# Graph attention and a small network on one core: 32 hidden outputs in column quarters of TensorE, half the heads of the last 23 tiles on DVE, and part of the network's start moved into those tiles

## The reference

```python
h = layernorm(x)
q, k, v = h @ Wq + bq, h @ Wk + bk, h @ Wv + bv        # 8 heads of 64
logits = sum_d(q[src] * k[dst]) / 8 + edge_bias        # rows = src, cols = dst
att = softmax of logits over the edges of one row
y = segment_sum(att * v[dst], src)
x = x + y @ Wo + bo
# the small network, two pipelines (add, sub), two positions
g = layernorm(x)                # 11 of its columns become features
r = relu(relu(f @ W0 + b0) @ W1 + b1) @ W2 + b2        # 160 wide, 2 outputs
x = x + (x + one-hot codes made of r at columns 128 to 160)
```

## Time and profile before

| | |
|---|---|
| median of 3 runs | 3393.04 us (3389.54 to 3396.01) |
| the profiled execution, its own time | 3388.5 us |
| its span, first to last instruction | 3386.7 us, mean granted TensorE clock 0.941 |
| busy | PE 2965.5, DVE 2891.4, ACT 2207.6, POOL 2206.9 us |
| sorting, projections | to some 1170 us |
| the tiles | to 2976 us |
| the network | to 3386.7 us |

### The profile page before, as it was taken

The page is one execution under the profiler, slowest core; times in us unless marked ns, Lnnn a source line. Parts: engine busy times, 40 slices in busy tenths (PEclk is TensorE's granted clock), DMA queues, the critical chain, the costliest instruction groups (busy, mean ns, idle before and its releaser), DMA issues.

```text
span 3386.7 us, 50546 instructions
## 1 busy us (share of the span) xinstructions
PE 2965.5 (88%) x11485; PEld 1732.4 (51%) x11610; DVE 2891.4 (85%) x8827; ACT 2207.6 (65%) x7734; POOL 2206.9 (65%) x2509
## 2 busy tenths in 40 slices
PE   6898888888887369999999999999999999889998
PEld 4554544544554135555555555555555555445554
DVE  9897777777776379999999999999999999867776
ACT  6332222222221059999999999999999999934443
POOL 0377777777777557777777777777777777511110
PEclk9898888888898689999999999999999999999999
DMA  6343333333332688878888887888888888411121
GB/s 205 81 135 102 106 107 100 102 101 107 104 104 67 224 287 256 253 253 254 256 257 254 257 259 252 258 258 253 257 256 252 257 256 259 145 66 69 68 70 55
DMA packets 258890, 615.16 MB, mean 182 GB/s; under 512 B 69451, under 2 KB 80023, under 8 KB 258338
## 3 DMA queue, kind: packets, MB, share of 16 engines
q0 software_dynamic: 144832, 443.72, 41.5%
q1 hardware_dynamic: 107414, 155.39, 15.1%
q10 hardware_dynamic: 6348, 12.80, 1.1%
HBM read 550.28 MB, written 61.49 MB: 181 GB/s over the span
## 4 chain that ended last, share of the span: by engine, by line
POOL 26%; DVE 25%; issue 20%; PE 14%; DMA 8%; ACT 3%; DVEq 2%; another core or an unknown queue 1%; ACTq 0%; SPq 0%; POOLq 0%
POOL rec_scratch L617 22%; DMA big<-kv_scratch,small 8%; DVE big L1374 6%; PE banks L1920 5%; DVE small L1272 5%; DVE big L1266 5%; PE banks L1949 4%; POOL big L638 3%; ACT big L799 3%; POOL small L645 2%; DVE big L992 2%; PE banks L1963 1%; PE banks L1874 1%; PE banks L1823 1%
## 5 line engine op out<-in xcount | busy, mean ns | idle before, releaser
L799 ACT ACTIVATE big<-big,small 128x65 f32<-128x65 f32 x6656 | 1625.9, 339 | 4.8
L638 POOL DMA_INDIRECT big<-kv_scratch,small x832 | 842.8, 1013 | 405.6 <-DVE small L1272 285.7
L617 POOL DMA_INDIRECT rec_scratch<-big,small x782 | 770.0, 985 | 340.4 <-issue 237.9
L1874 PE MATMUL banks<-big,small 128*128 128x260 f32 x3328 | 898.4, 393 | 96.1 <-POOL small L645 42.7
L1823 PE MATMUL banks<-big,small 128*128 x1664 | 876.5, 609 | 30.7 <-DMA big<-q_scratch 12.0
L1874 PEld LDWEIGHTS banks<-big,small 128*128 128x128 f32 x3328 | 597.4, 190 | 534.4 <-ACT big L799 243.0
L1374 DVE SCALAR_TENSOR_TENSOR big<-big,loS,banks 128x520 f32 x832 | 611.4, 735 | 20.2 <-PE banks L1874 18.6
L1731 PE MATMUL banks<-big 128*128 128x512 f32 (+1 forms) x1176 | 609.5, 666 | 19.5 <-DVE big L982 19.5
L1266 DVE TENSOR_TENSOR big<-banks,big 128x512 f32<-128x512 f32 x832 | 558.6, 671 | 43.9 <-PE banks L1823 25.7
L645 POOL TENSOR_SCALAR small<-iotaF,small 128x128 f32<-128x128 f32 x832 | 524.3, 630 | 54.1 <-PE banks L1874 28.2
L1272 DVE TENSOR_REDUCE small<-big 128x8 f32<-128x512 f32 x832 | 548.4, 664 | 0.0
(11 more groups left out here) (257 smaller groups left out, 2742.1 us busy)
## 6 DMA issues: line engine op xcount, KB each, us to landing
rowR<-lo_rows SPq DMA_DIRECT2D x97, 256.0 KB
big<-src_rows SPq DMA_DIRECT2D x97, 256.0 KB, 3.6
big<-in_x_dram SPq DMA_DIRECT2D x96, 256.0 KB, 2.8
big<-kv_scratch,small POOLq DMA_INDIRECT x832, 5.2
rec_scratch<-big,small POOLq DMA_INDIRECT x782
kv_scratch<-big SPq DMA_DIRECT2D x48, 260.0 KB
q_scratch<-big SPq DMA_DIRECT2D x48, 256.0 KB
kv_scratch<-big SPq DMA_DIRECT2D x48, 256.0 KB
```

What stands on the lines that cost most here:

```text
L617: e.indirect_dma_start(recd, bass.IndirectOffsetOnAxis(ap=ridx[:, c % 4, j:j + 1], axis=0), rec[:, 8 * c + j, :], None).then_inc(s_sc[c % ...
L638: e.indirect_dma_start(KV[:, vat(t):vat(t) + YW + D], None, KVd, bass.IndirectOffsetOnAxis(ap=recB[b_ % 4][:, t % 16, 9:10].bitcast(i32), ...
L799: ins = e.activation(heads(Vr(t), h, h + 1), heads(Vr(t), h, h + 1), ACT.Copy, scale=ph[:, h:h + 1])
L1874: ins = e.matmul(YB[t % 2][:, i, :], oh[t % 4], Vr(t)[:, 260 * i:260 * i + 260], start=True, stop=True)
```

## The change

1. **Last 32 outputs.** Part two of layer two is made as four products of 128 columns for each weight, each into 32 partitions of bank 5 (the column quarters of the array). So `h2[1]` holds all four groups at partitions 32 j, ACT's relu there has 128 columns instead of 512, and the weights of the outputs, `N2t`, have one block of four columns for each quarter with zeros elsewhere (1114 columns of `fwd` instead of 1102, six more `wload`).
2. **Last 23 tiles (809 to 831).** ACT scales heads 4 to 7 (`HV = 4`); heads 0 to 3 are one DVE product of 128x260 (`pv`), and `yt` waits for both.
3. **The network begins in them.** `f_y` of windows 0 to 5, `f_yT` of 0 to 5, `f_yTe` of 0 to 4, `f_xb` of 0 to 3, `f_wo` and `f_x1` of 0 and 1 are put at fixed steps of the tiles' loops. `f_wo` of 2 and 3 stay behind the last tile. SP loads after `yt` of tile 809. The network's buffers are laid into slots of the k and v ring that are free by then.

Three products of 512 columns became twelve of 128 columns with 32 outputs. The diff, cut to its core:

```diff
-        fwd = dram("network_weights", (128, 1102), f32)
+        fwd = dram("network_weights", (128, 1114), f32)
+        LAST = T - DEL
+        HV = 4
...
-                wload(W2t[0:32, 4 + 2 * pi_:6 + 2 * pi_], wT[2, 128:160, 100:102])
+                for j in range(4):
+                    wload(W2t[32 * j:32 * j + 32, 4 + 4 * j + 2 * pi_:6 + 4 * j + 2 * pi_], wT[2, 128:160, 100:102])
...
 (SP)
-            q.wait_ge(s_ya, T)
-            q.wait_ge(s_yt, T)
-            q.wait_ge(s_pva, T)
-            e.dma_start(fw2, fwd).then_inc(s_fw, 16)
-            e.dma_start(WoS, wo.rearrange("(c p) n -> p c n", p=128)).then_inc(s_wo, 16)
-            for w in range(XR):
-                f_load(w)
+            q.wait_ge(s_yt, T - 22)
+            q.wait_ge(s_rd, T)
+            q.wait_ge(s_pr, T)
+            f_load(0)
...
+            f_load(1)
+            f_load(2)
+            f_load(3)
+            e.dma_start(fw2, fwd).then_inc(s_fw, 16)
+            f_load(4)
+            f_load(5)
+            f_load(6)
+            q.wait_ge(s_yt, T - 20)
+            f_load(7)
...
 (POOL)
+                if s - T in (10, 13, 16, 19):
+                    f_xb((10, 13, 16, 19).index(s - T))
...
 (ACT)
-                for h in range(8):
+                for h in range(HV if t >= LAST else 0, 8):
...
+                if s - T in (10, 12, 16, 19, 22):
+                    f_yTe((10, 12, 16, 19, 22).index(s - T))
...
+                    e.activation(h2[1][0:C // 4, 0:128], BK[5][0:C // 4, 0:128], ACT.Relu).then_inc(s_h2r, 1)
...
 (DVE)
+            def pv(t):
+                v = Vr(t)[:, 0:65 * HV].rearrange("p (h d) -> p h d", d=65)
+                q.wait_ge(s_ex, t // 16 + 1)
+                e.tensor_tensor(v, v, pB[t // 16 % 2][:, t % 16, 0:HV].rearrange("p (h a) -> p h a", a=1).broadcast_to([128, HV, 65]), ALU.mult).then_inc(s_pvv, 1)
...
+                if LAST <= s - DEL < T:
+                    pv(s - DEL)
+                if s - T in (7, 8, 11, 13, 17, 20):
+                    f_y((7, 8, 11, 13, 17, 20).index(s - T))
+                if s - T in (15, 18):
+                    f_x1((15, 18).index(s - T))
...
-            for w in pair(0) + pair(1) + pair(2):
-                f_y(w)
-            for w in pair(0):
-                f_x1(w)
...
 (PE)
+                q.wait_ge(s_pvv, t - LAST + 1)
...
+                if s - T in (8, 10, 14, 17, 20, 23):
+                    f_yT((8, 10, 14, 17, 20, 23).index(s - T))
+                if s - T in (12, 15):
+                    f_wo((12, 15).index(s - T))
...
+                    for j in range(C // 128):
+                        ins = e.matmul(BK[5][32 * j:32 * j + 32, 0:128], lw[:, 128:160], h1[i][:, 128 * j:128 * j + 128],
+                                       start=(i == 0), stop=(i == 2))
...
+                        e.matmul(BK[7][0:n, 4 * j:4 * j + 4], h2[0][:, c0:c0 + n], N2t[:, 0:4], start=True, stop=False)
+                        ins = e.matmul(BK[7][0:n, 4 * j:4 * j + 4], h2[1][:, 0:n], N2t[:, 4 + 4 * j:8 + 4 * j], start=False, stop=True)
...
+            f_wo(2)
+            f_wo(3)
             f_fq(0)
```

More of the change, by code:

```diff
@@ L863, in _ @@
             q.wait_ge(s_ya, T)
[L864 to L868 removed]
+            q.wait_ge(s_fw, 39 * 16)
+            f_yTe(5)
             for w in pair(0):
                 f_root(w)
[L871 to L872 removed]
             f_FT(0)
```

184 lines of the change are left out of this document (89 added, 95 removed).

## The result

| | before | changed |
|---|---|---|
| median of five runs | 3391.49 us | 3328.2 us |
| lowest to highest | 3387.93 to 3396.01 | 3319.16 to 3330.37 |
| ratio | | 0.9815, 95% interval 0.9802 to 0.9827 |
| profiled execution, its span | 3388.5, 3386.7 | 3330.37, 3328.5 |

The change takes 63 us off, 1.9%. The time is inside the predicted range (3322 to 3377) and 13 us under the predicted 3341. The two profiled spans differ by 58.2 us, and four landmarks on DVE split that. All of them are in the traces: the last reduces of the tiles, the last addition into the windows' sums, the second pair's statistics, the end.

What follows compares the result with a forecast made beforehand. Bounds: ACT in the last tiles, waits among engines at the network's start, then PE in the iterations. 3388.5 - 2.5 - 24.0 - 25.4 = 3336.6 us, carried over to a median of 3341 us; range 3322 to 3377.

Steps and rivals of the forecast that it cites:

- b): Network's start: 9.7 us instead of 33.7 from last addition to second pair's statistics, 24.0 us gained.
- c): Last 32 outputs of layer two in column quarters: 1.53 us instead of 2.57 an iteration, 25.4 us gained.
- 12 x 0.107: Short passes of the 32 outputs: one product's second pass overlaps the next's first, so 1.28 us.
- rival 1: 32 outputs: all four quarters side by side, 6 x 0.107 + 0.25 = 0.9 us; kernel 3325.6 us; chance 0.18.
- PE's closest pace: Objection to all four quarters side by side: 0.055 us a load and product, so 24 are already 1.3 us.
- the change of shape: 32 outputs: entering and leaving another array shape costs 0.25 us, taken between 0 and 0.34.
- my 14.5: Forecast length in us of one network iteration after the change.
- a): Last 23 tiles: moving work from ACT to DVE and starting the network there ends the last addition 2.5 us sooner.
- POOL's four additions are covered: Last tiles: POOL runs up to four tiles ahead of its 1.4 us bias additions, so one 1.4 us is covered.
- d): Program's start: six more tiny weight loads on SP, 0.28 us each, cost nothing; without cover 1.7 us.
- rival 2: 32 outputs: no overlap, loads hidden, 2.57 + 0.25 us, a loss of 6.1; kernel 3372.6 us; chance 0.18.
- rival 3: 32 outputs: every quarter pays its weight load, 4.9 us, 57 lost; kernel 3419, median 3423.5 us; chance 0.08.

Runs made afterwards that it cites:

- experiment 9: The changed kernel run again, unaltered; ratio 0.9816 to the kernel before.
- experiment 10: Changed kernel with one output product serving the second 32 outputs of all four row blocks instead of four products; ratio 0.9799 to the kernel before.
- experiment 11: Experiment 10's kernel with the two projections inside the tiles cut into four pieces, one a tile, and DVE's two additions moved behind them; 3522.7 us, ratio 0.9777.
- experiment 12: Experiment 11's kernel run once more on another chip; ratio 0.977, 77.5 us under the kernel before.
- experiment 1: Kernel before with only the last 32 outputs in column quarters, with their weight layout, relu and six loads; 3352.2 us against 3391.1, ratio 0.9886.
- experiment 3: Changed kernel with all 24 short passes sent to the same quarter of the array; 3367.4 us in one run, iteration 15.83 us.
- experiment 5: Changed kernel with the four short products in two column quarters instead of four; 3557.9 us in one run on a slower chip, iteration 14.53 us.
- experiment 6: Changed kernel with 64 columns instead of 128 in each of the 24 short passes; 3548.5 us in one run on a slower chip, iteration 13.58 us.
- experiment 4: Changed kernel with the short products reordered, all three of one quarter and then of the next; 3339.9 us in one run, iteration 14.61 us.
- experiment 7: Changed kernel with POOL's first four output-bias additions cut to one column instead of 512; ratio 0.9813 to the kernel before.
- experiment 2: Changed kernel with layer two as it was before, leaving the last tiles' and network start's changes; 3365.05 us, ratio 0.9926.

## Why the prediction was right, and where it was not

**b) The network's start: right.** 24.0 us predicted, 24.05 in the trace; 9.64 or 9.65 us from the last addition to the second pair's statistics in experiments 9 to 12 too. DVE's own work was the length, and PE's two kept projections lay beside it. The clock stood at 1.00 where it had been 0.80.

**c) The 32 outputs: the mechanism was right, the degree was wrong.** 25.4 us predicted, 38.9 measured by experiment 1. What failed is the count "12 x 0.107": I let only the second pass of one product run with the first of the next. In the order of the change six passes of a quarter are the whole stream, 6 x 0.107, as rival 1 had it; experiments 3, 5 and 6 carry this, and four passes begin together in the changed trace. My objection to rival 1, that PE's closest pace was 0.055 us for a load and a product, was no bound: 24 took 0.79 us, 0.033 each. The bound of rows with other shapes of array was taken for that of the issue. Two terms held: 0.107 us for a pass, and the change of shape, 0.25 taken and 0.31 measured. The Trainium skill, TensorEngine Tiling (Array Packing), Key Properties, says that tiles load and multiply independently, and that a change of mode drains the engine; both agree with this case, the first by 0.95 us against 2.88, the second by 0.31 us, though no run here parts a drain from whatever else the change of shape costs. That the order of experiment 4 gives 14.61 us, near my 14.5, is coincidence: in that order six passes in a row need the same quarter, and by my pairing it would take 15.3.

DVE's features did not become the bound: they are ready 0.74 us before PE wants them where it was 2.4, and in experiment 10 0.53, with PE still waited for at 13.22 us.

**a) The last 23 tiles: wrong in sign, and small.** 2.5 us sooner was predicted, 0.4 to 3.6 later came (drains of 46.6 to 49.8 against 46.2). The length of the product (0.43) and the two waits hold: 2.36 and 0.78, 3.1 us where I had 3.8. ACT bounds no more, as said, but its last activations end at 2970.8 and not near 2955: it stands 12.5 us behind PE's transposes, in front of the five copies, which I had counted only with their 0.5 us. What failed is the sentence that POOL's four additions are covered because POOL runs ahead. POOL had the room, but DVE did not: a product of DVE with both inputs in the same memory as POOL's stood until POOL was done. In experiment 7 that goes away, and with it 2.5 us of DVE's part (43.0 in experiment 5, 40.5), of which 1.0 is given back to the wait: 46.57 to 45.07. The rest of my sum was near: 43.7 us of drain less 3.8 of waits is 39.9 for DVE's part, and the 40.5 of experiment 7 still hold the last two products at 0.83 us. The changed kernel's own 48.67 has some 2 us more than experiment 5, from the long first normalisation and the fall of PE's clock behind it; neither was in the sum. The sign was in the trace before, where I did not look for it: under POOL's addition

```profile
2985.64 10.28 POOL L669 TENSOR_TENSOR big<-big,small 128x512 f32<-128x512 f32 x8 [17.55 <-DMA big<-in_x_dram]
```
```profile
2992.51 1.06 DVE L1495 TENSOR_TENSOR big<-big 128x512 f32<-128x512 f32 x1 [8.77 <-PE banks L1910]
2993.50 1.23 DVE L1488 TENSOR_SCALAR big<-big 128x8 f32<-128x8 f32 x1
...
2995.00 1.47 DVE L1495 TENSOR_TENSOR big<-big 128x512 f32<-128x512 f32 x1
```

DVE's normalisation took 1.06 and 1.47 us instead of 0.69, and an operation on eight columns with one input 1.23. The Trainium skill, SBUF — State Buffer (SBUF: two separate sides), has the rule: an operation of DVE with two inputs there and one of POOL that reads there take one pair of ports in turn, each for a whole instruction. The trace agrees: 1.3 to 1.4 us against 0.42, while the additions of 128x520, which read one input from the accumulators, kept 0.74 to 0.76 throughout. Why the operation with one input was long too, no run here settles. Had I weighed the rule, four additions at up to 1.0 us each would have put a) at 0 to +1.5.

**d) Six more loads: nothing, as far as can be seen.** The last reduces come at 2932.06 and 2931.87 (experiment 1), but at 2929.24, 2929.41 and 2929.96 in experiments 2 to 4, which have the same six loads; before had 2929.77. So the 2.3 us of the table of stretches are within the chance of one profiled execution, and no cost of the loads can be told from it. The loads were not undone alone.

The sum thus came out 13 us high. Trace against trace it was 6.2 high (3336.6 against 3330.4): 13.5 in c), less 5.0 in a) and 2.3 before it. The rest is where the profiled executions lie: 4.5 us under the median before, 2.2 over the one after. Some 2 us of the drain and 3.6 at the end are the clock and the first normalisation in this one profile, so a luckier profile would have lain further from my sum. That the time fell inside the range is owed to rival 1, which the range held; my own term for c) was 13.5 us short. Rival 1, to which I had given 0.18, came true in its mechanism and in its iteration (13.9 us). Rivals 2 and 3 fell: rival 2's iteration, 15.8 us, is that of experiment 3 (15.83), where the overlap was taken away, and no weight load shows there, since 24 of them with nothing beside them cost 0.31 us together with the change of shape.

## What to carry to other kernels

Where a product leaves columns of the array empty, cut its moving rows into blocks and give each block its own quarter, in an order that goes round the quarters: the price here is 0.31 us each time the shape changes and changes back, and the stream shrinks with the number of quarters. Then look at what the new layout allows: the four blocks stacked on the partitions let one product replace four. Before POOL is given work with two inputs because "it has room", ask what DVE does in those microseconds. Work of PE that is put between tiles does better in pieces, one a tile, with what waits for it moved behind the last piece (2.2 us here, the two not run apart). And before a few microseconds are read from one profile, look at the granted clock in that stretch: the same kernel showed drains of 47.4 and 48.7 us and ends of 20.6 and 24.3.

## What the runs showed of the hardware that I had not expected

- 24 passes with 24 weight loads in 0.79 us, 0.033 us each, in four column quarters; half the columns take them to 0.48 (3304.79 to 3305.27 in experiment 6).
- The order matters by degrees: three products of a quarter in a row cost 0.71 us more than going round, neither none nor all of the overlap. Two quarters' passes are under way 0.25 us after the first.
- Of two short products behind a projection the first costs 0.14 us and the second 0.23, so that taking out three of the second kind gave 0.68 us where 0.45 was expected.
- The same drain took 46.6 to 49.8 us in eight traces. POOL's first addition, started by the landing of x, met DVE's 512-column normalisation in four of them, and PE's clock was at its lower level for part of five. Either alone goes with 0.7 to 1.0 us more, both with 2.1 and 3.2. What makes the clock fall in some executions and not in others, these runs don't show.
